# First attention of a hybrid layer on one Trainium2 core: order of the square roots, the scan's top by doubling passes, x summed in PSUM, search constants made earlier

## The chip, the core and the metric

The kernel runs on one core of one Trainium2 chip. Its time is the device time of one execution in microseconds (us), measured over several runs. Next to it stands one profiled execution, from which all rows below are taken. A core has five engines with a queue each: PE (TensorE, matrix multiply, with its weight loads shown as PEld), DVE (VectorE), ACT (ScalarE), POOL (GpSimd) and SP (SyncE, which only issues DMAs). Each runs its own list of instructions in order, and they meet only through semaphores.

## The reference

x has the shape (2, 2048, 128). Four layers are added to it in turn: a first attention with a complex linear recurrence, an expert layer, a linear attention, and the expert layer again; each sees the layer norm of x. The change touches only the first:

```
a2 = (xf @ w_a.T).reshape(b, l, inner, 2)
a_mag2 = a2[..., 0] ** 2 + a2[..., 1] ** 2
a = complex(a2) * (rsqrt(a_mag2) * sigmoid(log(a_mag2)))
xc = complex(x2) * (rsqrt(x_mag2) * x_mag2)
u = einsum('mn,bln->blm', inv(V), roll(xc, h0))
_, s = associative_scan(combine, (a, a * u), axis=1)    # s[t] = a[t] * s[t-1] + a[t] * u[t]
h = einsum('mn,bln->blm', V, s) + xc
x = x + h.real @ w_out.T
```

The expert layer that follows needs a layer norm of the new x, so mean and variance of every row, and a search for the 256 tokens of each expert, which walks over the bits of a threshold.

## The kernel before, in words

Sizes in the code: NB = 2 sequences of LT = 2048 positions, D = 128, INNER = 64, GW = 512 positions per block, NK = 4 blocks, NG = 8 groups of 512 rows of x, LEVELS = 11. The recurrence is laid out with one channel per partition (64 channels of each sequence, 128 partitions) and time along the free dimension; real and imaginary part are planes of one tile. `av` holds a, `XC` holds xc, `SS` the scan's values, `lev` the products of a over 2, 4, 8, ... positions.

Startup: x is loaded (`load_x`), VectorE makes the statistics, `scales` turns them into mean and 1/deviation, and `norm_a` normalises 32 tiles (L1056). After that VectorE does `coefficients(k)` for the four blocks (L1098 to L1021).

Block loop (NK times): TensorE projects a block (L770, two halves), with one step of a Newton iteration for the inverse of V in between (`inverse`). ScalarE copies the projection out of PSUM (L562, `raw`), runs its part of the inverse (L531, L535, L539, L541), keeps the next block's transposed x (`keep_xT`, L521) and squares (L569). `roots(k-1)` (L553) takes the square roots of the magnitudes of the block before; it is called after the first half's copy and `keep_xT`. VectorE's `coefficients(k)` waits for `squared`, adds squares to magnitudes (L1098, `mag_ready`), makes a reciprocal (L1101), waits for `rooted`, and multiplies; the last product raises `proj_used`.

GpSimd forms the products of a by pairs (`level`, L395 to L398): two levels for each block (`BY_BLOCK`), then levels 3 to 10 over the whole length. A level is four instructions: two with a pair of planes each, two with one plane. A block's levels wait for `proj_used` of the block and `mag_ready` of the next one. Every level raises `lev_ready`.

After the coefficients VectorE makes the search's constants (`bits`, ten small instructions, L1021 and L1025, each waiting for the one before). Then comes the scan. `times` is its complex product: two products of two planes each, a subtraction and an addition of one plane, and, where it adds to what is there, one addition of two planes; five instructions of L1021 in that case. First five chunks (two of 256 positions, three of 512) make the lowest level out of u, which TensorE puts into PSUM (L796 to L799). Then levels 1 to 10 go up the tree, and 9 to 0 down it, each as one `times` or two. Level n has LT / 2^(n+1) products. The last one, level 0 going down, has 1023, in two parts of 512 and 511; each part raises `s_ready`.

Way out: for eight groups of 256 positions TensorE adds up in PSUM bank n the contribution of xc (first loop, `way_out(.., 2, ..)`, started once `u_used` is complete) and of the scan (second loop, L807, waiting for `s_ready`, 1 for the first four groups and 2 for the others), and raises `ao_ready`. VectorE adds each group to x (`row`, `xs`), raises `x1_ready`, and makes four statistics (L1175). SP waits for all of `x1_ready` before it stores x for the expert layer.

What each line number stands for in the rows: L1021 is the helper `tt`, any two-input operation of VectorE; L1025 and L1026 are the helper `ts`. A float32 matmul shows as two passes (x2).

Of the kernel before, what the change touches and what calls it, by code (L numbers as in the profile page):

```python
# [10 lines left out]
ALU = mybir.AluOpType  # L11
# [26 lines left out]
def build(nc, x, wa, wx, wo, vr, vi, vrT, viT, h0r, h0i, wqkvT, woutT, nw, rwT, rb, f1T, f1b, f2T, f2b, out):  # L38
# [30 lines left out]
    with ExitStack() as ctx:  # L69
# [45 lines left out]
        rt2 = tbf[:, 2 * GW:4 * GW].rearrange("p (c t) -> p c t", c=2)  # L115
        rec = tbf[:, 4 * GW:5 * GW]

        MB = tbf[:, 3600:3600 + 3 * 2 * D].rearrange("p (i b d) -> p i b d", i=3, b=NB)
        T1 = sq[:, 0:2, :]
        T2 = sq[:, 2:4, :]  # L120
# [133 lines left out]
        AT_ROOT, AT_FIRST, AT_STEP = 8, 12, 6  # L254

        BY_BLOCK = 2
        lv_at = [0] * (LEVELS + 1)
        for lv in range(2, LEVELS):
            lv_at[lv] = lv_at[lv - 1] + (LT >> (lv - 1))
# [88 lines left out]
        def _(pool):  # L348
# [38 lines left out]

            scratch = stage.rearrange("p j d -> p (j d)")

            def level(A, B, n):  # L390
# [3 lines left out]
                even, odd = A[:, :, 0::2], A[:, :, 1::2]  # L394
                G.did(pool.tensor_tensor(t1, odd[:, 0:1, :].to_broadcast([P, 2, n]), even, ALU.mult))  # L395
                G.step(pool.tensor_tensor(t2, odd[:, 1:2, :].to_broadcast([P, 2, n]), even, ALU.mult))
                G.did(pool.tensor_tensor(B[:, 0, :], t1[:, 0, :], t2[:, 1, :], ALU.subtract))
                pool.tensor_tensor(B[:, 1, :], t1[:, 1, :], t2[:, 0, :], ALU.add).then_inc(lev_ready, 1)  # L398
                G.settle()

            for k in range(NK):

                pool.wait_ge(proj_used, k + 1)
                if k + 1 < NK:
                    pool.wait_ge(mag_ready, k + 2)
                pool.wait_ge(transposed, min(2 * (k + 2), NG))
                A = av[:, :, k * GW:(k + 1) * GW]
                for i in range(BY_BLOCK):
                    n = GW >> (i + 1)
                    B = lev[:, :, lv_at[i + 1] + k * n:lv_at[i + 1] + (k + 1) * n]  # L410
                    level(A, B, n)
                    pool.wait_ge(lev_ready, k * BY_BLOCK + i + 1)
                    A = B
            for lv in range(BY_BLOCK + 1, LEVELS):
                n = LT >> lv
                level(lev[:, :, lv_at[lv - 1]:lv_at[lv - 1] + 2 * n], lev[:, :, lv_at[lv]:lv_at[lv] + n], n)
                pool.wait_ge(lev_ready, level_done(lv))

            def feed(f):

# [84 lines left out]
        def _(act):  # L505
# [51 lines left out]
                keep_xT(0, b, b * NK)  # L557
            for k in range(NK):
                at = AT_FIRST + AT_STEP * k
                for i, raw in enumerate((av[:, :, k * GW:(k + 1) * GW], XC[:, :, 1 + k * GW:1 + (k + 1) * GW])):  # L560
                    act.wait_ge(projected, 2 * k + i + 1)
                    nc.scalar.activation(raw, ps[:, 2 * i:2 * i + 2, :], ACT.Copy).then_inc(raw_ready, 1)  # L562
                    inverse(at + 2 * i + 1)
                    if k + 1 < NK:
                        keep_xT(0, 2 * (k + 1) + i, i * NK + k + 1)
                    if i == 0 and k >= 1:
                        roots(k - 1)
                    act.wait_ge(raw_ready, 2 * k + i + 1)
# [15 lines left out]
            for b, r in enumerate((lo_, hi_)):  # L584
                nc.scalar.activation(MB[r, 0, b, :], ps[r, 7, 0:D], ACT.Copy)
                last = nc.scalar.activation(MB[r, 1, b, :], ps[r, 7, D:2 * D], ACT.Copy, scale=-1.0)
            last.then_inc(mt_ready, 1)

            def feed(f):
                run = 1 + 2 * f  # L590
# [111 lines left out]
        def _(pe):  # L702
# [107 lines left out]
            for n in range(2 * NK):  # L810
                for t in range(2):
                    at = (2 * n + t) * P + 1
                    way_out(n, t, 2, XC[:, 0, at:at + P])
            for n in range(2 * NK):
                pe.wait_ge(s_ready, 1 if n < NK else 2)
                for t in range(2):
                    at = (2 * n + t) * P
                    for i in range(2):
                        last = way_out(n, t, i, SS[:, i, at:at + P])
                last.then_inc(ao_ready, 1)  # L820
# [196 lines left out]
        def _(dve):  # L1017
# [91 lines left out]

            for k in range(NK):  # L1110
                norm_a(k)
            for k in range(NK):
                coefficients(k)
            def times(cr, ci, n, q, o, add_to, done=None, count=0):
# [15 lines left out]
                    V.step(tt(to[:, 1, :], t1[:, 1, :], t2[:, 0, :], ALU.add))  # L1130


            dve.wait_ge(consts, 3)
            V.step(tt(bits[:, 0:32], ione[:, :], ish[:, :], ALU.logical_shift_left))
            low, shifted = bits[:, 32:33], bits[:, 33:34]
            V.step(tt(low, bits[:, 1:2], bits[:, 2:3], ALU.bitwise_or))
            for by in (2, 4, 8, 16):
                V.step(ts(shifted, low, by, None, ALU.logical_shift_right))
                V.step(tt(low, low, shifted, ALU.bitwise_or))
            for c, (t0, w) in enumerate(U_CHUNKS):  # L1140
                H = w // 2
                dve.wait_ge(u_ready, c + 1)
# [5 lines left out]
                tt(v, SS[:, :, e], U[:, :, 1::2], ALU.add).then_inc(u_used, 1)  # L1148
                dve.wait_ge(u_used, c + 1)
                times(av[:, 0:1, o], av[:, 1:2, o], H, v, SS[:, :, o], False)  # L1150
            for lv in range(1, LEVELS):
                s, n = 1 << lv, LT >> (lv + 1)
                dve.wait_ge(lev_ready, level_done(lv))
                A = lev[:, :, lv_at[lv]:lv_at[lv] + 2 * n]
                for c0 in range(0, n, GW):
                    w = min(GW, n - c0)
                    q = SS[:, :, s - 1 + c0 * 2 * s::2 * s][:, :, 0:w]
                    o = SS[:, :, 2 * s - 1 + c0 * 2 * s::2 * s][:, :, 0:w]
                    times(A[:, 0:1, 2 * c0 + 1::2][:, :, 0:w], A[:, 1:2, 2 * c0 + 1::2][:, :, 0:w], w, q, o, True)
            for lv in range(LEVELS - 2, -1, -1):  # L1160
                s, n = 1 << lv, (LT >> (lv + 1)) - 1
                A = lev[:, :, lv_at[lv]:lv_at[lv] + 2 * (n + 1)] if lv else av
                for c0 in range(0, n, GW):
                    w = min(GW, n - c0)
                    q = SS[:, :, 2 * s - 1 + c0 * 2 * s::2 * s][:, :, 0:w]
                    o = SS[:, :, 3 * s - 1 + c0 * 2 * s::2 * s][:, :, 0:w]
                    times(A[:, 0:1, 2 * c0 + 2::2][:, :, 0:w], A[:, 1:2, 2 * c0 + 2::2][:, :, 0:w], w, q, o, True,
                          s_ready if lv == 0 else None, c0 // GW + 1)
# [282 lines left out]
```

## Time and profile before

| | us |
|---|---|
| median of 3 runs | 735.89 (734.93 to 737.31) |
| the profiled execution | 735.69 |
| its span | 733.9 |
| busy: PE, DVE, POOL, ACT | 410.8, 461.8, 355.6, 205.2 |

The profile's span is the time from the first to the last instruction of the program; the execution's time has a little around it. In a row of the chain or of the timeline the first number is the start in us from the span's start, the second how long it took (several instructions when "xN" stands behind it), then the engine, the tile written and the source line. In the chain a piece is listed until the next piece takes over.

### The profile page before, as it was taken

To read this page: it belongs to the slowest core of one execution; us is meant where nothing else is said; L and a number is where in the kernel's file an instruction comes from. 1 tells how busy PE (TensorE), PEld (TensorE's weight loads), DVE (VectorE), ACT (ScalarE), POOL (GpSimd) and SP (SyncE) were. 2 spreads that over 40 slices of the span, in tenths; PEclk is the share of its full clock that TensorE was granted. 3 is DMA by queue.
4 is the path that set the end of the run, shared out by engine and by line. 5 is a ranking of instruction groups with operands and counts; after the bars stand their busy time and mean duration, and the time that the engine had idled before them with its cause. 6 is when DMAs were issued, how large, how long until landed. Compare 5 with 4: busy or idle time off the path is not lost.

```text
span 733.9 us, 7537 instructions
## 1 busy us (share of the span) xinstructions
PE 410.8 (56%) x2130; PEld 273.7 (37%) x2130; DVE 461.8 (63%) x1199; ACT 205.2 (28%) x487; POOL 355.6 (48%) x350
## 2 busy tenths in 40 slices
PE   4887560084231396674057888887753313975650
PEld 4554140072110286664023433433331102965540
DVE  6779999997778322222439899999777783222210
ACT  2575000003440142222064334333234401422210
POOL 5048930002000478887308788888720004688853
PEclk9999886589555599998559899999975555999885
DMA  5950000006002523334700000000060024233322
GB/s 139 364 225 0 0 1 0 0 0 172 0 0 52 136 51 47 45 38 64 201 0 0 1 0 2 0 1 0 1 171 1 0 60 130 40 46 44 45 23 18
DMA packets 49860, 38.91 MB, mean 53 GB/s; under 512 B 8672, under 2 KB 46176, under 8 KB 48544
## 3 DMA queue, kind: packets, MB, share of 16 engines
q1 hardware_dynamic: 36000, 28.30, 12.6%
q0 software_dynamic: 11392, 9.05, 9.3%
q10 hardware_dynamic: 2432, 1.11, 0.6%
q8 instruction: 17, 0.28, 0.2%
q14 instruction: 19, 0.16, 0.1%
HBM read 22.73 MB, written 15.73 MB: 52 GB/s over the span
## 4 chain that ended last, share of the span: by engine, by line
DVE 27%; POOL 22%; issue 17%; DMA 15%; PE 13%; ACT 4%; SPq 1%; DVEq 1%; ACTq 0%; POOLq 0%
DVE arena L1021 10%; POOL tb L501 8%; DMA out<-arena,idx 5%; DMA acc<-arena,idx 5%; POOL acc L455 4%; POOL out L455 4%; POOL arena L442 3%; DVE tk L1026 2%; PE ps L807 2%; DVE arena L1026 2%; PE ps L770 2%; DVE tb L1056 2%; DMA tab<-tb 2%; PE ps L855 2%; POOL arena L497 1%
## 5 line engine op out<-in xcount | busy, mean ns | idle before, releaser
L1021 DVE TENSOR_TENSOR arena<-ps,arena 128x256 f32<-128x256 f32 (+1 forms) x36 | 16.4, 454 | 139.6 <-DMA acc<-arena,idx 59.5
L615 ACT ACTIVATE arena<-ps,b 128x256 f32<-128x256 f32 x128 | 50.1, 474 | 143.7 <-PE ps L907 143.7
L501 POOL TENSOR_TENSOR tb<-arena 128x512 f32<-128x512 f32 x64 | 80.4, 1270 | 17.2 <-DVE arena L1369 17.2
L954 PE MATMUL ps<-xT,arena 128*128 128x512 f32 x128 | 71.7, 654 | 20.7 <-DVE arena L1369 20.6
L907 PE MATMUL ps<-arena,f1w 128*128 128x256 f32 x256 | 73.3, 438 | 17.6 <-DVE arena L1025 12.7
L442 POOL DMA_INDIRECT arena<-tab,idx x64 | 62.6, 978 | 41.5 <-DMA tab<-tb 22.6
L917 PEld LDWEIGHTS ps<-f2w,arena 128*128 128x128 f32 x512 | 64.2, 197 | 4.4 <-issue 2.2
L917 PE MATMUL ps<-f2w,arena 128*128 128x128 f32 x512 | 63.9, 279 | 2.0 <-DVE arena L1025 2.0
L907 PEld LDWEIGHTS ps<-arena,f1w 128*128 128x128 f32 x256 | 53.8, 221 | 27.4 <-DVE arena L1025 14.4
L455 POOL DMA_INDIRECT out<-arena,idx x32 | 50.9, 1590 | 23.5 <-issue 10.5
L271 POOL DMA_DIRECT2D arena<-cntd x4 | 2.7, 687 | 117.3 <-DMA cntd<-arena 117.3
L1021 DVE TENSOR_TENSOR arena<-arena 128x256 f32<-128x256 f32 (+26 forms) x127 | 57.8, 490 | 2.6
L455 POOL DMA_INDIRECT acc<-arena,idx x32 | 50.6, 1580 | 9.7 <-issue 7.0
L807 PE MATMUL ps<-tb,arena 128*128 128x256 f32 x96 | 25.4, 433 | 44.1 <-DVE arena L1021 37.8
L423 POOL CAST arena<-ident 128x128 f16<-128x128 f32 x2 | 0.6, 289 | 83.1 <-DVE tb L1056 83.1
L1026 DVE TENSOR_SCALAR_CACHE_REDUCE arena<-arena,tk 128x320 f16<-128x320 f32 (+1 forms) x66 | 37.1, 564 | 4.7 <-DVE tk L1026 2.1
L807 PEld LDWEIGHTS ps<-tb,arena 128*128 128x128 f32 x96 | 21.1, 222 | 48.8 <-DVE arena L1021 38.2
L604 ACT ACTIVATE arena<-arena,tk 128x192 f16<-128x192 f32 x60 | 27.3, 455 | 42.2 <-DVE tk L1026 40.0
L954 PEld LDWEIGHTS ps<-xT,arena 128*128 128x128 f32 x128 | 22.1, 205 | 45.5 <-DVE arena L1369 38.2
L517 ACT ACTIVATE sd<-sd 128x32 f32<-128x32 f32 x4 | 0.9, 227 | 133.5 <-DVE sd L1044 133.5
L1369 DVE TENSOR_TENSOR_SCAN arena<-ones,arena,ps 128x512 f32<-128x512 f32 x30 | 37.3, 1261 | 0.0
L891 PE MATMUL ps<-ident,arena 128*128 128x128 f32 x64 | 14.4, 311 | 37.8 <-DMA arena<-tab,idx 29.9
(230 smaller groups left out, 936.8 us busy)
## 6 DMA issues: line engine op xcount, KB each, us to landing
tab<-tb SPq DMA_DIRECT2D x8, 576.0 KB, 5.7
f1w<-in_f1T SPq DMA_DIRECT2D x4, 1024.0 KB, 12.5
f2w<-in_f2T SPq DMA_DIRECT2D x4, 1024.0 KB, 14.3
acc<-tb SPq DMA_DIRECT2D x8, 256.0 KB, 18.7
arena<-in_f2b SPq DMA_DIRECT2D x2, 1024.0 KB, 6.0
acc<-xs SPq DMA_DIRECT2D x8, 256.0 KB, 6.5
xs<-acc SPq DMA_DIRECT2D x8, 256.0 KB, 5.8
arena<-acc SPq DMA_DIRECT2D x8, 256.0 KB, 5.4
```

The lines of the kernel that those rows point to most:

```text
L442: pool.indirect_dma_start(out=XE[:, e % RX, h, :], out_offset=None, in_=tab[f], in_offset=bass.IndirectOffsetOnAxis(ap=idx[:, i:i + 1], ax ...
L455: pool.indirect_dma_start(out=outf if f else acc[e % 2], out_offset=bass.IndirectOffsetOnAxis(ap=idx[:, i:i + 1], axis=0), in_=yv[:, e % 2 ...
L501: pool.tensor_tensor(QS[:, i, :], ST[:, r, i, :], qn[:, r, :], ALU.mult).then_inc(qs_ready, 1)
L604: nc.scalar.activation(eq[:, DCOL:GW], even[:, DCOL:GW], ACT.Sign, bias=tk[:, 0:1], scale=-1.0, accum_out=sg[:, 0:1]).then_inc(signed, 1)
L615: last = nc.scalar.activation(hT[:, e % 2, t, :], ps[:, 2 * (e % 2) + t // 2, (t % 2) * CAP:(t % 2 + 1) * CAP], ACT.Gelu, bias=b1[:, e, t: ...
L807: return nc.tensor.matmul(ps[:, n, t * 2 * D:(t + 1) * 2 * D], lhs, MB[:, i, :, :].rearrange("p b d -> p (b d)"), start=(i == 2 and t == 0 ...
L907: last = nc.tensor.matmul(ps[:, 2 * (e % 2) + t // 2, (t % 2) * CAP:(t % 2 + 1) * CAP], f1w[:, e, t * P:(t + 1) * P], xeT[:, e % 2, :], st ...
L917: last = nc.tensor.matmul(ps[:, 6 + m % 2, h * P:(h + 1) * P], hT[:, m % 2, t, h * P:(h + 1) * P], f2w[:, m, t, :], start=(t == 0), stop=( ...
L954: nc.tensor.matmul(ps[:, u % V_BANKS, :], WV[:, i, :, :].rearrange("p h a -> p (h a)"), xT[:, n * GW:(n + 1) * GW], start=True, stop=True) ...
L1021: return nc.vector.tensor_tensor(o, a, b, op)
L1026: return nc.vector.tensor_scalar(o, a, s1, s2, op0, op1, **kw)
L1369: nc.vector.tensor_tensor_scan(ST[:, r, i, :], ones_in.to_broadcast([P, GW]), kv, ST[:, 1 - r, i, GW - 1:GW] if n % NK else 0.0, ALU.mult, ...
```

## The change

Four edits.

- ScalarE: `roots(k-1)` is called ahead of the copy of a block's first half, where it was called behind it.
- VectorE: the search's constants are made behind `norm_a`, ahead of `coefficients`, where they were made behind these.
- The scan's top: with TOP = 6 there are NTOP = 32 values left. VectorE goes up by levels 1 to 5, then makes five passes with strides 1, 2, 4, 8, 16 over the 32 values (widths 31, 30, 28, 24, 16), then down by levels 5 to 0. GpSimd makes levels 3 to 6, and then the coefficients of the passes in four steps, kept in `over_top`. The last level (0, down) is cut into four parts of 256 and 255, and `s_ready` counts to four.
- The way out: a matmul of the identity with the rows of x joins each group and half in the first loop. ScalarE copies the finished groups out of PSUM over x and raises `x1_ready`; VectorE only makes the statistics.

```
@@ gpsimd
-            for lv in range(BY_BLOCK + 1, LEVELS):
+            for lv in range(BY_BLOCK + 1, TOP + 1):
                 n = LT >> lv
-                level(lev[:, :, lv_at[lv - 1]:lv_at[lv - 1] + 2 * n], lev[:, :, lv_at[lv]:lv_at[lv] + n], n)
+                A = lev[:, :, lv_at[lv - 1]:lv_at[lv - 1] + 2 * n]
+                level(A[:, :, 0::2], A[:, :, 1::2], lev[:, :, lv_at[lv]:lv_at[lv] + n], n)
                 pool.wait_ge(lev_ready, level_done(lv))
+            for j, d in enumerate(STRIDES[:-1]):
+                A = over_top[j]
+                level(A[:, :, d:NTOP - d], A[:, :, 2 * d:NTOP], over_top[j + 1][:, :, 2 * d:NTOP], NTOP - 2 * d)
+                pool.wait_ge(lev_ready, level_done(TOP + j + 1))
@@ scalar
+                if k >= 1:
+                    roots(k - 1)
                 for i, raw in enumerate((av[:, :, k * GW:(k + 1) * GW], XC[:, :, 1 + k * GW:1 + (k + 1) * GW])):
                     act.wait_ge(projected, 2 * k + i + 1)
                     nc.scalar.activation(raw, ps[:, 2 * i:2 * i + 2, :], ACT.Copy).then_inc(raw_ready, 1)
                     inverse(at + 2 * i + 1)
                     if k + 1 < NK:
                         keep_xT(0, 2 * (k + 1) + i, i * NK + k + 1)
-                    if i == 0 and k >= 1:
-                        roots(k - 1)
...
+            for n in range(2 * NK):
+                act.wait_ge(ao_ready, n + 1)
+                nc.scalar.activation(xrows[:, :, 2 * n:2 * n + 2, :], ps[:, n, :].rearrange("p (t b d) -> p b t d", t=2, b=NB),
+                                     ACT.Copy).then_inc(x1_ready, 1)
@@ tensor
                     way_out(n, t, 2, XC[:, 0, at:at + P])
+                    nc.tensor.matmul(ps[:, n, t * 2 * D:(t + 1) * 2 * D], ident[:, :], xrows[:, :, 2 * n + t, :],
+                                     start=False, stop=False, skip_group_check=True)
             for n in range(2 * NK):
-                pe.wait_ge(s_ready, 1 if n < NK else 2)
+                pe.wait_ge(s_ready, n // 2 + 1)
@@ vector (the ten instructions on bits, between norm_a and coefficients now)
...
-            for lv in range(1, LEVELS):
+            for lv in range(1, TOP):
...
-            for lv in range(LEVELS - 2, -1, -1):
+            for j, d in enumerate(STRIDES):
+                dve.wait_ge(lev_ready, level_done(TOP + j))
+                w, s, A = NTOP - d, 1 << TOP, over_top[j]
+                ends = SS[:, :, s - 1::s]
+                times(A[:, 0:1, d:], A[:, 1:2, d:], w, ends[:, :, 0:w], ends[:, :, d:], True)
+            for lv in range(TOP - 1, -1, -1):
...
-                for c0 in range(0, n, GW):
-                    w = min(GW, n - c0)
+                part = GW if lv else GW // 2
+                for c0 in range(0, n, part):
+                    w = min(part, n - c0)
...
             for n in range(2 * NK):
-                dve.wait_ge(ao_ready, n + 1)
-                row = xs[:, :, :].rearrange("p (b j) d -> p b j d", b=NB)[:, :, 2 * n:2 * n + 2, :]
-                tt(row, row, ps[:, n, :].rearrange("p (t b d) -> p b t d", t=2, b=NB), ALU.add).then_inc(x1_ready, 1)
                 dve.wait_ge(x1_ready, n + 1)
```

## Rows read from the trace of the kernel before

**Rows 1.** The page, part 4: shares of the chain that ended last, by engine.
```profile
DVE 27%; POOL 22%; issue 17%; DMA 15%; PE 13%; ACT 4%; SPq 1%; DVEq 1%; ACTq 0%; POOLq 0%
```

**Rows 2.** Chain of waits in time, 64 to 79 us: start, us, engine, tile, line.
```profile
64.50 1.39 DVE tb L1098
...
74.05 0.37 DVE bits L1021
...
78.92 0.76 DVE arena L1021 x2
```

**Rows 3.** Windows: stretch, length, PE, PEld, DVE, ACT, POOL busy (instructions), PEclk, DMA, GB/s.
```profile
28.70:33.07 4.37, 3.73 (x24) 2.21 (x20) 0.00 (x0) 3.40 (x8) 0.00 (x0) 1.00 1.02 424
...
74.90:98.50 23.60, 12.91 (x24) 5.10 (x24) 22.67 (x43) 0.00 (x0) 21.45 (x40) 0.86 0.00 0
```

**Rows 4.** Timeline, all engines, 24 to 39 us; in brackets idle time before, and releaser.
```profile
24.41 1.94 PE L770 MATMUL ps<-xT,waT 128*64 128x512 f32 x8 [0.78 <-ACT xT L521]
...
33.07 1.23 DVE L1098 TENSOR_TENSOR tb<-arena 128x1024 f32<-128x1024 f32 x1 [4.38 <-ACT arena L569]
...
35.09 1.94 PE L770 MATMUL ps<-xT,waT 128*64 128x512 f32 x8
35.19 0.28 ACT L541 ACTIVATE XX<-ps 128x128 f32<-128x128 f32 x1
...
37.07 1.02 ACT L562 ACTIVATE arena<-ps 128x1024 f32<-128x1024 f32 x1 [1.60 <-PE ps L770]
...
38.63 1.06 ACT L553 ACTIVATE tb<-tb 128x1024 f32<-128x1024 f32 x1
```

**Rows 5.** Groups by form, VectorE, 73.9 to 103.9 us: busy us, mean ns, idle.
```profile
L1021 DVE TENSOR_TENSOR bits<-bits 128x1 uint32<-128x1 uint32 x5 | 3.5, 710 | 0.2
...
L1025 DVE TENSOR_SCALAR bits<-bits 128x1 uint32<-128x1 uint32 x4 | 0.6, 154 | 0.1
```

**Rows 6.** Timeline of VectorE: chunks 0, 1 and 4, and one small instruction.
```profile
81.26 1.93 DVE L1021 TENSOR_TENSOR arena<-arena,tb 128x256 f32<-128x256 f32 x2
...
84.69 0.75 DVE L1021 TENSOR_TENSOR arena<-arena,ps 128x256 f32<-128x256 f32 x2
...
99.20 1.29 DVE L1021 TENSOR_TENSOR arena<-arena,ps 128x512 f32<-128x512 f32 x2
100.52 0.76 DVE L1021 TENSOR_TENSOR arena<-arena 128x256 f32<-128x256 f32 x2
...
185.72 0.16 DVE L1021 TENSOR_TENSOR tk<-tk,bits 128x1 uint32<-128x1 uint32 x1
```

**Rows 7.** Chain of waits, the tree: level 1 up, 3 up, 5 up, 6 up, 5 down.
```profile
104.17 3.97 DVE arena L1021 x2
...
116.70 0.51 DVE arena L1021 x2
...
119.38 0.46 DVE arena L1021 x2
...
120.49 0.35 DVE arena L1021 x2
...
127.66 0.45 DVE arena L1021 x2
```

**Rows 8.** Chain of waits: last level going down, and the last statistics.
```profile
143.81 2.37 DVE arena L1021 x2
...
165.99 0.88 DVE bst L1175 x4
```

**Rows 9.** Windows: the first 4 us of the way out, columns as in rows 3.
```profile
148.80:152.80 4.00, 3.99 (x9) 3.20 (x10) 3.93 (x5) 0.00 (x0) 0.00 (x0) 0.50 0.00 0
```

**Rows 10.** Timeline: the way out's two loops on TensorE, a copy on ScalarE.
```profile
38.15 0.60 ACT L521 ACTIVATE xT<-ps 128x512 f32<-128x512 f32 x1
...
102.06 9.00 PE L807 MATMUL ps<-tb,arena 128*128 128x256 f32 x32 [6.31 <-DVE tb L1021]
148.81 16.42 PE L807 MATMUL ps<-tb,arena 128*128 128x256 f32 x64 [37.75 <-DVE arena L1021]
```

More of the change, by code:

```diff
@@ L116, in build @@
         rec = tbf[:, 4 * GW:5 * GW]
+        xrows = xs[:, :, :].rearrange("p (b j) d -> p b j d", b=NB)
         MB = tbf[:, 3600:3600 + 3 * 2 * D].rearrange("p (i b d) -> p i b d", i=3, b=NB)
@@ L256, in build @@
         BY_BLOCK = 2
+        TOP = 6
+        NTOP = LT >> TOP
+        STRIDES = [1 << j for j in range(NTOP.bit_length() - 1)]
+        over_top = [lev[:, :, sum(LT >> i for i in range(1, TOP)):][:, :, 0:NTOP]]
+        over_top += [tbf[:, 2560 + 2 * NTOP * j:2560 + 2 * NTOP * (j + 1)].rearrange("p (c t) -> p c t", c=2)
+                     for j in range(len(STRIDES) - 1)]
         lv_at = [0] * (LEVELS + 1)
@@ L388, in _, with level @@
             scratch = stage.rearrange("p j d -> p (j d)")
-            def level(A, B, n):
+            def level(even, odd, B, n):
                 t1 = scratch[:, 0:2 * n].rearrange("p (c t) -> p c t", c=2)
                 t2 = scratch[:, 2 * n:4 * n].rearrange("p (c t) -> p c t", c=2)
-                even, odd = A[:, :, 0::2], A[:, :, 1::2]
                 G.did(pool.tensor_tensor(t1, odd[:, 0:1, :].to_broadcast([P, 2, n]), even, ALU.mult))
@@ L410, in _ @@
                     B = lev[:, :, lv_at[i + 1] + k * n:lv_at[i + 1] + (k + 1) * n]
-                    level(A, B, n)
+                    level(A[:, :, 0::2], A[:, :, 1::2], B, n)
                     pool.wait_ge(lev_ready, k * BY_BLOCK + i + 1)
                     A = B
-            for lv in range(BY_BLOCK + 1, LEVELS):
+            for lv in range(BY_BLOCK + 1, TOP + 1):
                 n = LT >> lv
-                level(lev[:, :, lv_at[lv - 1]:lv_at[lv - 1] + 2 * n], lev[:, :, lv_at[lv]:lv_at[lv] + n], n)
+                A = lev[:, :, lv_at[lv - 1]:lv_at[lv - 1] + 2 * n]
+                level(A[:, :, 0::2], A[:, :, 1::2], lev[:, :, lv_at[lv]:lv_at[lv] + n], n)
                 pool.wait_ge(lev_ready, level_done(lv))
+            for j, d in enumerate(STRIDES[:-1]):
+                A = over_top[j]
+                level(A[:, :, d:NTOP - d], A[:, :, 2 * d:NTOP], over_top[j + 1][:, :, 2 * d:NTOP], NTOP - 2 * d)
+                pool.wait_ge(lev_ready, level_done(TOP + j + 1))
             def feed(f):
@@ L1111, in _ @@
                 norm_a(k)
+            dve.wait_ge(consts, 3)
+            V.step(tt(bits[:, 0:32], ione[:, :], ish[:, :], ALU.logical_shift_left))
+            low, shifted = bits[:, 32:33], bits[:, 33:34]
+            V.step(tt(low, bits[:, 1:2], bits[:, 2:3], ALU.bitwise_or))
+            for by in (2, 4, 8, 16):
+                V.step(ts(shifted, low, by, None, ALU.logical_shift_right))
+                V.step(tt(low, low, shifted, ALU.bitwise_or))
             for k in range(NK):
@@ L1130, in times @@
                     V.step(tt(to[:, 1, :], t1[:, 1, :], t2[:, 0, :], ALU.add))
[L1133 to L1139, printed above, removed]
             for c, (t0, w) in enumerate(U_CHUNKS):
@@ L1167, in _ @@
                     times(A[:, 0:1, 2 * c0 + 2::2][:, :, 0:w], A[:, 1:2, 2 * c0 + 2::2][:, :, 0:w], w, q, o, True,
-                          s_ready if lv == 0 else None, c0 // GW + 1)
+                          s_ready if lv == 0 else None, c0 // part + 1)
             for n in range(2 * NK):
-                dve.wait_ge(ao_ready, n + 1)
-                row = xs[:, :, :].rearrange("p (b j) d -> p b j d", b=NB)[:, :, 2 * n:2 * n + 2, :]
-                tt(row, row, ps[:, n, :].rearrange("p (t b d) -> p b t d", t=2, b=NB), ALU.add).then_inc(x1_ready, 1)
                 dve.wait_ge(x1_ready, n + 1)
```

## Prediction

> **What bounds the kernel now.** I read the page first. The chain of work that ended last is shared out over VectorE, GpSimd, DMA and TensorE [rows 1], so no engine bounds the whole and each edit has to be judged in its own stretch. All edits lie in the first attention, the first 167 us. So the second view is the chain of waits in order of time over that stretch. It shows the kernel changing its limit three times.
>
> Up to 64.5 us the block loop (projection, square roots, matrix inverse) sets the pace. TensorE starts a block's first projection at 24.41 and the next block's at 35.09, that is 10.68 us later [rows 4], and the two blocks behind follow at the same distance. From 64.5 to 148.8 us the chain is VectorE alone: coefficients of the last block, the search constants, five chunks of the scan's lowest level, and the tree up and down [rows 2, 7, 8]. From 148.8 to 165.3 it is TensorE's way out, 64 passes in 16.42 us [rows 10], and then one addition, four statistics instructions [rows 8] and the normalising. Behind that comes the first expert layer. Its search, gathers and scatters start from these statistics through semaphores alone, so I let what is won here pass through to the end one for one.
>
> **Square roots first in a block.** ScalarE ends block 0's last copy at 35.19 + 0.28 = 35.47 and then idles until the projection lands (copy at 37.07); today the root sits behind that copy, at 38.63 [rows 4]. The magnitudes it needs are done at 33.07 + 1.23 = 34.30 [rows 4]. After the change the root runs at 35.5 to 36.5, inside the idle time, 0.5 us before the copy is due. VectorE gets its roots some 2 us earlier. Its next multiplication can then start when the reciprocal ends (about 38.2 instead of 39.8). But the pace is not set there. Block 0 holds no root and takes the same 10.68 us as the blocks that hold one, and the last block's magnitudes start at 64.50 [rows 2], right behind ScalarE's squares, whatever VectorE did before. I cost this edit at **0**. What hides the root is the 1.6 us before the copy; without that cover each of three blocks would lose up to 1.06 us. The added head-of-line risk is ScalarE waiting for magnitudes with the copy, the inverse's copies and the kept xT queued behind it. The slack there is 35.47 - 34.30 = 1.2 us plus the 0.5 us.
>
> **Search constants behind the normalising.** Ten small VectorE instructions move from 74.05-78.92 [rows 2], where they are on the chain and cost 4.87 us, to the gap 28.70 to 33.07, where VectorE is wholly idle and so is GpSimd [rows 3]. Undisturbed, such an instruction takes 0.16 us [rows 6], with 0.02-0.03 us between, so ten take about 2.0 us and end near 30.7. They fit, and normalising is ahead of them.
>
> Taking them out does not return all 4.87 us. The instructions with two inputs took 710 ns on average and those with one 154 ns [rows 5], because GpSimd's tree levels run there; it is busy 21.45 us of 74.90-98.50 [rows 3]. Excess of the constants: 4.87 - 2.0 = 2.9 us. The chunks behind them suffer too. An undisturbed long chunk is 104.17 - 99.20 = 4.97 us [rows 6, 7]. A short one, from undisturbed pairs of the same widths (0.75, 0.51, half of 0.75, 0.76, 0.51 and five gaps of 0.02) [rows 6, 7], is 3.0. Five chunks undisturbed: 2 x 3.0 + 3 x 4.97 = 20.9. They took 104.17 - 78.92 = 25.25, so 4.35 us of excess; chunk 0 alone has 84.69 - 78.92 - 3.0 = 2.8 [rows 2, 6]. GpSimd's heavy work stays where it is in time (its last block starts only when GpSimd ends the one before), so the chunks move forward into it. Chunk 0 now meets what the constants met (I take 2.7 of their 2.9), chunk 1 what chunk 0 met (2.3 of 2.8, since more of it now reads PSUM while GpSimd's long instructions run), chunk 2 a part of what chunk 1 met (0.7). That is 5.7 us of excess, the chunks end at 74.05 + 20.9 + 5.7 = 100.65 instead of 104.17, and the edit brings **3.5 us**. Bounds: 4.87 if the chunks suffer no more than today, 2.0 if the whole 2.9 + 4.35 = 7.25 us stays lost. The pair that GpSimd hits hardest shows why it will not be the upper end: 1.93 us against 0.76 [rows 6].
>
> The Trainium skill (GPSIMD Engine Reference, Specifications) says GpSimd shares SBUF interfaces with VectorE and contends with VectorE instructions that read two SBUF inputs. By that rule, which the one-input rows bear out with their 154 ns, the edit pays less than the 4.87 us that the chain shows; taken as a full return the gain below would be 1.4 us larger.
>
> **The scan's top.** Levels 6 to 10 going up and 9 to 6 going down, nine in all, stand in the chain from 120.49 to 127.66, 7.17 us [rows 7]. They are small and cost their fixed part. Five doubling passes of width 31, 30, 28, 24 and 16 take their place, each of five instructions as a level has. The level of width 32 takes 120.49 - 119.38 = 1.11 us and the mean of the nine, of 16 and less, is 0.80 [rows 7]; between them I take 1.10 + 1.09 + 1.06 + 1.02 + 0.92 = 5.2. Gain **2.0 us**; bounds 1.6 (all at 1.11) and 3.2 (all at 0.80). On GpSimd four steps of width 30 to 16 replace four of 16 to 2. That ends near 99 as before [rows 3], while VectorE asks for the first of them at about 117, so it is hidden with 17 us to spare.
>
> **The last level in four parts.** Its first half takes 148.81 - 143.81 = 5.0 us [rows 8] and releases TensorE, which has been waiting. A quarter is two products of 512 elements (1.29), two halves of 256 (0.76), one addition of 512 (half of 1.29) and gaps: 2.8 us [rows 6]. TensorE starts **2.1 us** earlier against that clock. Four quarters cost VectorE 11.1 us instead of 9.9, but nothing waits for that: TensorE needs 4.1 us for the two groups of a quarter on average, and even in the faster part (16.42 - 4.0) / (64 - 9) x 16 = 3.6 us [rows 9, 10], more than 2.8, so it never starves. The statistics, 0.88 us a group [rows 8], catch up with 2 us a group. Bounds: 0 and 2.4.
>
> The skill speaks against this cut (VectorE: DVE Perf Modes, "The TRN2 errata"): each instruction pays a fixed latency, so tiles of 512 or more elements are advised. Ten more instructions are 1.2 us here, agreeing with the rule, and would count if VectorE were the limit of this stretch; then this part would lose 1.2 rather than win 2.1.
>
> **x summed by TensorE.** Sixteen matmuls, 32 passes, join the 32 of 102.06 [rows 10], at most at the same 9.0 us. They start near 98.6 and end by 117, and the quarter is ready at 141: 24 us of cover, without which they cost 9.0. The additions leave VectorE and eight ScalarE copies come in; a copy of 512 elements out of PSUM takes 0.60 [rows 10]. ScalarE has nothing queued but the root of the next statistics, which waits for them anyway. Only the last one counts. Today the last statistics start at 165.99, 0.76 behind the end of the way out at 148.81 + 16.42 [rows 8, 10]; then it is 0.60 and two hops of 0.03 to 0.05. **0**, bounds -0.2 to +0.2. Storing x starts at the same distance from the way out.
>
> **Sum.** 3.5 + 2.0 + 2.1 = 7.6 us. Against the profiled execution: span 733.9, time 735.69, giving 728.1; the median of the runs, 735.89, is 0.2 above it, so **728.2**.
>
> **The rivals.** (1) *The port keeps its whole toll*: the constants bring only 2.0; 5.5 to 6.1 in all, 729.8. For it: the excess belongs to GpSimd's 21 us more than to the victim. Against: part of a chunk reads PSUM and was not slowed. (2) *It returns all*: 4.9, with the top at its better end, 726.5. (3) *The early start is lost*: 730.3, if TensorE's first quarter meets the lower clock longer. In 148.80-152.80 its granted clock is 0.50, which is 1.2 GHz, behind 37.7 us without work [rows 9, 10]; the idle time will now be about 24 us, and I expect the same start. (4) *The roots hold up the blocks*: 3 x 1.06, 731.4; it decides once magnitudes come 1.7 us later than now. (5) *TensorE starves between quarters and stays at the lower clock*: 64 passes at 4.0/9 = 0.44 us are 28 us, which the boundary passes counted short make nearer 26, so 9 to 10 us lost, 737.5. It decides when a quarter takes over 3.6 us; it is estimated at 2.8 and GpSimd is idle then. This is also the case in which the quarters do not do what they say. (6) *Slower*: VectorE and GpSimd run strictly one after the other from 74 to 98.5. VectorE would lose up to GpSimd's 21.45 us instead of 5.7, 15.8 more: 744.0. It decides from about 10 us of excess more than I took. Today the excess is 7.25 in the same stretch with the same GpSimd work, which speaks against it.
>
> **How the numbers follow.** Forecast 0.58, (1) 0.16, (2) 0.09, (3) 0.05, (4) 0.02, together 0.90 faster by over 0.3% (2.2 us, about what a measurement of this kernel can tell from no change). (5) is within 0.3%: 0.06. (6) is slower: 0.04. The range takes in the bounds: all terms near their best, 4.9 + 2.7 + 2.4 = 10.0, gives 725.9; constants at 2.0 and no early start, 4.0, gives 731.9. Range 725.8 to 732.0, with (5), (6) and a little more outside.
>
> **What the profile after would show.** VectorE's ten constants at about 28.7-30.7, each two-input one near 0.16 us; roots in front of the projection's copy, blocks still 10.7 us apart and the last magnitudes at 64.5; chunks from 74.1 to 100.7; no level between widths 32 and 16 but five passes of about 1.05 us; way out starting 2.8 us after the last level does, near 141, and taking 16.4 us; last statistics ended near 159.2 instead of 166.9. It is wrong if the chunks end after 102.5, if the blocks are more than 10.9 us apart, if the way out has gaps between its groups, or if the stretch behind the statistics is not as long as before.

## The result and the profile after

The kernel before took 735.99 us in this comparison (median of 4), the changed one 728.89 (727.53 to 729.38). The ratio is 0.9887, with a 95% interval from 0.9866 to 0.9907: faster by 1.1%, or 7.1 us between the medians. The forecast was 728.2 with a range of 725.8 to 732.0.

The span of the profiled execution went from 733.9 to 727.2 us. The shares of the chain on the page after, where VectorE had 27% and TensorE 13% before [rows 1]:

```profile
span 727.2 us, 7592 instructions
...
DVE 24%; POOL 20%; issue 16%; PE 16%; DMA 14%; ACT 4%; SPq 2%; DVEq 1%; ACTq 0%; POOLq 0%
```

Three points are some 20 us, more than the edits moved, so the shares don't measure them. Most of TensorE's rise lies behind the statistics, in a stretch that is as long as before. Some of it lies ahead of the first chunk, where the chain below now names a matmul of u (L816) as what came last. VectorE's own last product was as late (71.93 + 1.64 = 73.57), and in experiment 7 the first chunk starts at 72.47, ahead of that matmul at 73.02. So VectorE's order still sets this start.

The chain of waits of the changed kernel (start, us, engine, tile, line; L1117 is the last block's magnitudes, L1040 VectorE's two-input helper, L824 the way out, L816 a matmul of u, L603 the new ScalarE copy, L1197 the statistics) answers rows 2, 7 and 8:

```profile
64.16 1.24 DVE tb L1117
...
72.98 0.45 PE ps L816 x2
73.49 0.75 DVE arena L1040 x2
...
101.19 3.98 DVE arena L1040 x2
...
118.70 0.44 DVE arena L1040 x2
...
138.91 1.30 DVE arena L1040 x2
...
141.79 16.45 PE ps L824 x64
158.25 0.61 ACT xs L603
158.86 0.03 issue
158.88 0.88 DVE bst L1197 x4
159.77 0.02 issue
159.79 0.47 DVE sd L1040 x3
```

Read as distances, these give the whole gain up to the statistics' last step (before it stood at 166.90, which is the 0.88 us piece of [rows 8] and a hop behind 165.99):

| stretch | before | after | difference | forecast |
|---|---|---|---|---|
| start to the last magnitudes | 64.50 | 64.16 | -0.34 | 0 |
| magnitudes to the end of the coefficients | 9.55 | 9.33 | -0.22 | 0 |
| constants (before only) and five chunks | 30.12 | 27.70 | -2.42 | -3.5 |
| level 1 up to the last level down | 39.64 | 37.72 | -1.92 | -2.0 |
| last level to the way out's start | 5.00 | 2.88 | -2.12 | -2.1 |
| way out | 16.42 | 16.43 | 0 | 0 |
| its end to `scales` | 1.67 | 1.57 | -0.10 | 0 |
| sum, at `scales` | 166.90 | 159.79 | -7.11 | -7.6 |
| `scales` to the end | 567.0 | 567.4 | +0.4 | 0 |

The 0.34 us at the start is no effect of the edits. The first 26 us are one program in both kernels, and the first block's first copy starts at 26.38 before and 26.04 after, so the 0.34 us is there already. The runs below show last magnitudes anywhere from 64.08 to 64.95. In the timeline after (columns as in [rows 6]) the constants stand in the gap and take 0.15 to 0.18 us each:

```profile
28.27 0.18 DVE L1040 TENSOR_TENSOR bits<-ione,ish 128x32 uint32<-128x32 uint32 x1
28.48 0.16 DVE L1040 TENSOR_TENSOR bits<-bits 128x1 uint32<-128x1 uint32 x1
28.68 0.15 DVE L1044 TENSOR_SCALAR bits<-bits 128x1 uint32<-128x1 uint32 x1
```

### The profile page after: what moved, and what is told of

Its sections match the earlier page's. It is cut to its first block, busy times and chain, and to the rows that moved or that the text cites. A ratio compares the mean times of both kernels' runs of the same rounds, so it can differ in the third digit from the quotient of the medians.

```text
span 727.2 us, 7592 instructions
## 1 busy us (share of the span) xinstructions
PE 415.1 (57%) x2162; PEld 278.8 (38%) x2162; DVE 456.2 (63%) x1181; ACT 210.2 (29%) x495; POOL 356.9 (49%) x350
## 4 chain that ended last, share of the span: by engine, by line
DVE 24%; POOL 20%; issue 16%; PE 16%; DMA 14%; ACT 4%; SPq 2%; DVEq 1%; ACTq 0%; POOLq 0%
DVE arena L1040 10%; POOL tb L513 8%; DMA out<-arena,idx 6%; POOL acc L467 4%; POOL out L467 4%; DMA acc<-arena,idx 4%; DVE tk L1045 2%; PE ps L926 2%; PE ps L824 2%; DVE arena L1045 2%; PE ps L787 2%; DVE tb L1075 2%; DMA tab<-tb 2%; PE ps L874 2%; PE ps L936 1%
## 5 line engine op out<-in xcount | busy, mean ns | idle before, releaser
L1040 DVE TENSOR_TENSOR arena<-ps,arena 128x256 f32<-128x256 f32 (+1 forms) x36 | 16.3, 454 | 140.0 <-DMA out<-arena,idx 58.9
L926 PE MATMUL ps<-arena,f1w 128*128 128x256 f32 x256 | 71.8, 431 | 17.4 <-DVE arena L1044 12.9
L973 PE MATMUL ps<-xT,arena 128*128 128x512 f32 x128 | 68.7, 631 | 20.1 <-DVE arena L1391 20.1
L1040 DVE TENSOR_TENSOR arena<-arena 128x256 f32<-128x256 f32 (+21 forms) x109 | 57.4, 560 | 2.2
L824 PE MATMUL ps<-tb,arena 128*128 128x256 f32 x96 | 27.0, 421 | 32.8 <-DVE arena L1040 27.1
L973 PEld LDWEIGHTS ps<-xT,arena 128*128 128x128 f32 x128 | 21.4, 197 | 43.6 <-DVE arena L1391 36.1
L824 PEld LDWEIGHTS ps<-tb,arena 128*128 128x128 f32 x96 | 20.2, 213 | 37.3 <-DVE arena L1040 27.5
L509 POOL TENSOR_TENSOR arena<-arena 128x512 f32<-128x512 f32 x24 | 30.5, 1271 | 5.8 <-ACT arena L691 5.6
```

Of the source, the lines that this page charges most:

```text
L509: pool.tensor_tensor(KV[:, j % 2, :], KV[:, j % 2, :], kn[:, r, :], ALU.mult).then_inc(kv_ready, 1)
L824: return nc.tensor.matmul(ps[:, n, t * 2 * D:(t + 1) * 2 * D], lhs, MB[:, i, :, :].rearrange("p b d -> p (b d)"), start=(i == 2 and t == 0 ...
L926: last = nc.tensor.matmul(ps[:, 2 * (e % 2) + t // 2, (t % 2) * CAP:(t % 2 + 1) * CAP], f1w[:, e, t * P:(t + 1) * P], xeT[:, e % 2, :], st ...
L973: nc.tensor.matmul(ps[:, u % V_BANKS, :], WV[:, i, :, :].rearrange("p h a -> p (h a)"), xT[:, n * GW:(n + 1) * GW], start=True, stop=True) ...
L1040: return nc.vector.tensor_tensor(o, a, b, op)
```

## The experiments

The expectations were written before the runs. Times are medians; the ratio is to the kernel before on the same chip. The spread from run to run of one kernel is 2 to 8 us, wider than most terms. It goes with TensorE's mean granted clock: of the 17 executions of the kernel before that stand beside experiments 1 to 4, the five shortest (734.7 to 736.0 us) had 0.784 to 0.788 and the five longest (738.5 to 739.6) had 0.773 to 0.780. No run of the changed kernel stands beside the experiments, so against it the ratios are compared, and two such ratios leave some 2 us open either way. That can't decide between most of the theories below. The traces decide, in the distances of the table. From the last magnitudes to `scales` the changed kernel has 95.63 us and the kernel before 102.40.

**1. Constants back behind the coefficients** (the wait and the ten instructions on `bits`), all else as changed.

```
             for k in range(NK):
                 norm_a(k)
-            dve.wait_ge(consts, 3)
-            ...
             for k in range(NK):
                 coefficients(k)
...
+            dve.wait_ge(consts, 3)
+            ...
             for c, (t0, w) in enumerate(U_CHUNKS):
```

> The changed kernel with the ten search constants back behind the coefficients. Theory (the chunks moved forward into GpSimd's heavy work and pay its toll in the constants' place): the stretch from the last coefficient to level 1, 27.7 us in the changed kernel, becomes about 30.1, so 2.4 us slower than the changed kernel. Rival A, that the constants' whole 4.9 us came back and something else took 2.5: 4.9 slower, some 32.6 us. Rival B, that the gap they were put in was not free: under 1.5.

733.88 us, ratio 0.9951 (0.9932 to 0.9970). Last coefficient to level 1: 104.59 - 74.26 = 30.33 us, against 27.70. So the constants are worth 2.6 us there, not 4.9. The time alone would have spoken for rival A: by the ratios this kernel is 4.7 us behind the changed one. From the magnitudes to `scales` the trace has 3.3 of them. Besides the 2.6, another 0.6 us came from a way out of 17.06 us instead of 16.43. This is a difference of TensorE's low-clock start, told of below, and not of the edit.

**2. Square roots back behind the copy.**

```
             for k in range(NK):
                 at = AT_FIRST + AT_STEP * k
-                if k >= 1:
-                    roots(k - 1)
...
                         keep_xT(0, 2 * (k + 1) + i, i * NK + k + 1)
+                    if i == 0 and k >= 1:
+                        roots(k - 1)
```

> The changed kernel with the square roots again behind the copy and the kept xT. Theory: blocks stay 10.69 us apart, the last magnitudes start 31.36 us behind the second block's (64.16 - 32.80 in the changed kernel), the reciprocal is followed by 1.6 us of idle VectorE, and the time moves by 0 to 0.3 us. Rival (the root in front of the copy costs or wins block time): 1 to 3 us either way, with another distance between blocks.

730.78 us, ratio 0.9904 (0.9881 to 0.9927). That interval overlaps the changed kernel's. The timelines of both on ScalarE show the same pace, 10.69 and 10.70 us from the projection's copy of one block to the next (L574 and L576). First this run, with the root (L565) behind the copy, then the changed kernel:

```profile
37.16 1.02 ACT L574 ACTIVATE arena<-ps 128x1024 f32<-128x1024 f32 x1 [1.60 <-PE ps L787]
38.72 1.06 ACT L565 ACTIVATE tb<-tb 128x1024 f32<-128x1024 f32 x1
...
47.85 1.03 ACT L574 ACTIVATE arena<-ps 128x1024 f32<-128x1024 f32 x1 [1.60 <-PE ps L787]
```

```profile
35.03 1.05 ACT L565 ACTIVATE tb<-tb 128x1024 f32<-128x1024 f32 x1
36.73 1.02 ACT L576 ACTIVATE arena<-ps 128x1024 f32<-128x1024 f32 x1 [0.66 <-PE ps L787]
...
47.43 1.02 ACT L576 ACTIVATE arena<-ps 128x1024 f32<-128x1024 f32 x1 [0.42 <-PE ps L787]
```

The root only used up ScalarE's idle time before the copy, 1.60 down to 0.66 us. Magnitudes to `scales` is 95.83 us here, 0.2 more than the changed kernel. Most of that is a last magnitudes instruction of 1.38 us instead of 1.23, which GpSimd's block before still met.

**3. The last level in two parts.**

```
-                part = GW if lv else GW // 2
+                part = GW
...
-                pe.wait_ge(s_ready, n // 2 + 1)
+                pe.wait_ge(s_ready, n // 4 + 1)
```

> The changed kernel with the last level of the scan in parts of 512 and 511 and TensorE waiting for two of them. Theory: the way out starts 5.0 us behind the level's start where it is 2.88, takes the same 16.4, and the kernel is 2.1 us slower. Rival (the quarter's start is taken back, since TensorE starts at the lower clock anyway and is then held up by VectorE's longer level): under 0.7 slower, with a way out of over 17 us in the changed kernel's place.

732.51 us, ratio 0.9935 (0.9919 to 0.9952). The way out starts 143.85 - 138.84 = 5.01 us behind the level's start and takes 16.79. From the level's start to `scales` it is 23.37 us against 20.88, so 2.1 us of start and 0.4 of a longer start at the lower clock. The first theory holds. The ratios say 3.5 us, with the uncertainty above.

**4. x added by VectorE again**, quarters kept.

```
-                    nc.tensor.matmul(ps[:, n, t * 2 * D:(t + 1) * 2 * D], ident[:, :], xrows[:, :, 2 * n + t, :], ...)
...
-                act.wait_ge(ao_ready, n + 1)
-                nc.scalar.activation(xrows[:, :, 2 * n:2 * n + 2, :], ps[:, n, :]..., ACT.Copy).then_inc(x1_ready, 1)
...
+                dve.wait_ge(ao_ready, n + 1)
...
+                tt(row, row, ps[:, n, :]..., ALU.add).then_inc(x1_ready, 1)
                 dve.wait_ge(x1_ready, n + 1)
```

> The changed kernel with x added by VectorE again, no identity matmuls and no ScalarE copies. Theory: TensorE's last pass still sets the end; only the tail behind it differs, 0.69 us of addition for 0.60 of copy and a hop, so 0.0 to 0.1 us slower. Rival (with the quarters VectorE's 11.4 us level plus eight groups of 1.6 us is 24 us, longer than 2.9 + 16.4): the tail becomes VectorE's, about 4 to 5 us slower than the changed kernel. The rival follows from the sum of the rows and would make this edit a part without which the quarters win nothing.

733.65 us, ratio 0.9949 (0.9928 to 0.9969), by the ratios 4.6 us behind the changed kernel. The rival holds in kind: VectorE is the last. Its timeline (L1034 addition, L1194 statistics), the first group and the last two:

```profile
150.36 0.69 DVE L1034 TENSOR_TENSOR xs<-xs,ps 128x512 f32<-128x512 f32 x1
151.08 0.87 DVE L1194 BATCH_NORM_STATS2 bst<-xs 128x6 f32<-128x128 f32 x4
...
159.34 0.67 DVE L1034 TENSOR_TENSOR xs<-xs,ps 128x512 f32<-128x512 f32 x1
160.04 0.87 DVE L1194 BATCH_NORM_STATS2 bst<-xs 128x6 f32<-128x128 f32 x4
160.83 0.67 DVE L1034 TENSOR_TENSOR xs<-xs,ps 128x512 f32<-128x512 f32 x1
161.53 0.87 DVE L1194 BATCH_NORM_STATS2 bst<-xs 128x6 f32<-128x128 f32 x4
```

No idle time stands between them; TensorE was through at 141.83 + 16.04 = 157.87. From the level's start (138.95) to `scales` (162.44) it takes 23.49 us. In the kernel before, with halves, it is 23.09, and in the changed kernel 20.88. So the quarters alone would win nothing, and the x edit is worth 2.6 us with them. The rival's 4 to 5 was too high for two reasons: a group takes 1.50 us and not 1.6, and the last group's share of VectorE stands behind TensorE's line too. Up to the last group VectorE needs 11.4 + 7 x 1.5 = 21.9 us and TensorE 2.9 + 16.4 = 19.3, and the difference is the 2.6. The profiled execution lost another 2.7 us behind `scales` (570.1 against 567.4). The windows there, first the changed kernel, then this one at the same distance behind `scales`, show a lower granted clock (0.97 and 0.87, the third number from the end):

```profile
409.80:459.80 50.00, 43.08 (x182) 20.64 (x182) 47.85 (x68) 21.93 (x42) 42.13 (x34) 0.97 0.00 1
```

```profile
412.40:462.40 50.00, 44.93 (x178) 20.35 (x178) 45.83 (x65) 19.53 (x36) 38.83 (x33) 0.87 0.00 1
```

Why it was lower stays open; no experiment shows an edit's hand in it.

**5. The plain tree back**, quarters kept: `TOP`'s passes out, `range(1, LEVELS)` and `range(LEVELS - 2, -1, -1)` on VectorE, GpSimd's levels to 10.

> The changed kernel with the plain tree again (levels 1 to 10 up, 9 to 0 down, GpSimd's levels 3 to 10), quarters and the rest kept. Theory: four small levels more, the stretch from level 1 to the last level 39.6 us where it is 37.7, so 1.9 slower. Rival (the passes also spare something on GpSimd or behind): over 3 or under 1 slower.

737.55 us on a chip where the kernel before took 742.64; ratio 0.9935 (0.9917 to 0.9952), which in this ratio is 3.5 us behind the changed kernel. The trace puts level 1 to the last level at 141.09 - 101.44 = 39.65 us, that is 1.93 more. The stretch from magnitudes to `scales` is 96.63 us, only 1.0 more, as its way out took 15.70. What the ratio has beyond that is not in the attention; it is about what two ratios leave open, and no trace here explains it.

**6. The kernel before with only the constants moved.**

> The kernel before with only the ten search constants moved behind the normalising. Theory: the stretch from the last coefficient to level 1 goes from 30.1 to about 27.6, so 2.5 us faster than before and no more, though the chain of before showed 4.87 us on them. Rival A: 4.9 faster. Rival B (needs the roots first): under 1 faster.

739.87 us, ratio 0.9955 (0.9938 to 0.9973), 3.3 us faster. Last coefficient to level 1: 101.95 - 74.44 = 27.51 us against 30.12, so 2.6. Together with experiment 1 and the table, the move is worth 2.4 to 2.6 us in this stretch, with or without the other edits. Rival A is out, and so is rival B.

**7. GpSimd fills zeros where it made products** (the products of a are left out, so the scan is another).

```
             def level(even, odd, B, n):
-                ...
+                pool.memset(B, 0.0).then_inc(lev_ready, 1)
```

> The changed kernel, where GpSimd fills each level's result with zeros in one instruction in place of four products; the products of a are left out, so the scan's result is another. Theory (GpSimd's products hold up VectorE's two-input instructions): the five chunks take 20.9 us where they take 27.7, and the multiplications of the coefficients 1.23, 0.69 and 1.23 where they take 1.5, 1.2 and 1.6. Rival (the chunks are long by themselves, or by TensorE's reads): above 25 us. The kernel is 7 to 9 us faster by the first theory.

One execution, 727.95 us; the kernel before takes 742.64 on that chip. The chunks run from 72.47 to 93.53, 21.06 us, against 27.70. The groups by form between 73 and 93 us show which instructions were held. First the changed kernel, then this one (us busy, mean ns):

```profile
L1040 DVE TENSOR_TENSOR arena<-arena 128x128 f32<-128x128 f32 x8 | 4.7, 630 | 0.1
L1040 DVE TENSOR_TENSOR arena<-arena,tb 128x256 f32<-128x256 f32 x4 | 3.7, 965 | 0.1
...
L1040 DVE TENSOR_TENSOR arena<-arena,ps 128x512 f32<-128x512 f32 x4 | 2.6, 685 | 0.1
```

```profile
L1036 DVE TENSOR_TENSOR arena<-arena,ps 128x512 f32<-128x512 f32 x6 | 3.9, 684 | 0.1
...
L1036 DVE TENSOR_TENSOR arena<-arena 128x128 f32<-128x128 f32 x8 | 2.0, 289 | 0.1
L1036 DVE TENSOR_TENSOR arena<-arena,tb 128x256 f32<-128x256 f32 x4 | 1.5, 422 | 0.1
```

With both inputs in SBUF, an instruction of 256 elements falls from 965 to 422 ns and one of 128 from 630 to 289. With one input in PSUM it stays at 685 and 684. So the 6.6 us are GpSimd's products'. The filling itself held up nothing: between 72.66 and 74.97 it ran beside pairs of 0.49 and 0.76 us, which are undisturbed values (line L402, then VectorE).

```profile
72.66 2.31 POOL L402 MEMSET arena<- 128x512 f32 x6 [5.78 <-issue]
...
73.25 0.49 DVE L1036 TENSOR_TENSOR arena<-arena 128x128 f32<-128x128 f32 x2
...
74.24 0.76 DVE L1036 TENSOR_TENSOR arena<-arena,tb 128x256 f32<-128x256 f32 x2
```

The coefficients' multiplications fell too, from 1.49, 1.21 and 1.64 us to 1.23, 0.68 and 1.22.

**8. The same, with the constants back.**

> The same, GpSimd filling zeros (the products of a left out), and the ten search constants behind the coefficients again. Theory: they take 2.0 us there, 0.16 each, so the stretch from the last coefficient to level 1 is 22.9 us against 20.9. Rival (the constants are slow for what they are): 4.9 us.

729.88 us in one execution. The constants start at 72.37 and the first chunk at 74.32, 1.95 us; the chunks end at 95.38.

```profile
72.79 0.15 DVE L1040 TENSOR_SCALAR bits<-bits 128x1 uint32<-128x1 uint32 x1
72.98 0.16 DVE L1036 TENSOR_TENSOR bits<-bits 128x1 uint32<-128x1 uint32 x1
```

Without GpSimd's products the constants cost 2.0 us where the chain of before gave them 4.87.

**9. Passes one level lower** (TOP = 5: 64 values, six passes; their coefficients in a place of `tbf` that is free by then).

> The changed kernel with the passes one level lower (64 values, six passes of width 63, 62, 60, 56, 48 and 32, levels 1 to 4 around them). Theory (a pass costs what a level of its width costs, read from the rows): levels 5 up and down, 2.2 us, and five passes, 5.15, are replaced by six passes of 8.1 to 8.4, so the stretch from level 1 to the last level is 0.8 to 1.1 us longer than 37.7 and the kernel up to 1 us slower. Rival (instructions cost a flat 0.2 us and their number counts, five fewer): 0.5 faster.

732.71 us, ratio 0.9939 (0.9914 to 0.9963). Level 1 to the last level: 140.54 - 101.86 = 38.68 us, 0.96 more than the changed kernel, as the first theory has it. The stretch from magnitudes to `scales` is 97.78 us, 2.15 more, and by the ratios the kernel is 3.8 us behind, more than the theory's 1. A pass costs what a level of its width costs; the count of instructions alone does not set it. The chunks became 0.6 us longer too (28.33), which I hadn't expected: up to 91 us both timelines are alike, and then GpSimd's wider steps, which now end at 101.54 and not at 98.89, fall into the last two chunks. The other 0.6 us is a way out of 17.00.

**10. The first quarter halved.**

```
+                cuts = [0, 128, 256, 512, 768, n] if lv == 0 else list(range(0, n, GW)) + [n]
...
-                pe.wait_ge(s_ready, n // 2 + 1)
+                pe.wait_ge(s_ready, n + 1 if n < 2 else n // 2 + 2)
```

> The changed kernel with the first quarter of the last level cut once more, parts of 128, 128, 256, 256, 255, TensorE's first two groups waiting for one part each. Theory: a part of 128 takes 1.8 us, so the way out starts 1.8 behind the level's start where it is 2.9, and the time falls by 1.1 us. Rival (TensorE starves behind the first part or VectorE becomes the limit by its level and statistics, 12.0 + 7.2 = 19.2 against 1.8 + 16.4 + 1.5 = 19.7): under 0.5.

728.91 us, ratio 0.9883 (0.9860 to 0.9906): no difference from the changed kernel that this can tell. The way out started 141.01 - 139.20 = 1.81 us behind the level's start, as expected, but took 16.82 us, so 0.7 us is left at `scales`. TensorE did not starve, as its 64 passes stand in the timeline without a gap; its clock rose later. In the sixth microsecond of the way out (146.01 to 147.01) the granted clock is 0.72, where the changed kernel has 1.00 from the start of its sixth (146.79) on.

**11. Level 3 block by block, and no wait for the next magnitudes.**

```
-        BY_BLOCK = 2
+        BY_BLOCK = 3
...
-                if k + 1 < NK:
-                    pool.wait_ge(mag_ready, k + 2)
```

> The changed kernel with GpSimd making level 3 block by block too, and starting a block without waiting for the next one's magnitudes. Theory (the toll is GpSimd's two-input work in the stretch of the chunks, and some of it can lie earlier): GpSimd has 2.7 us less to do behind 74 us, the chunks end 0.5 to 1.5 us earlier; GpSimd's third block meets the last block's magnitudes, up to 0.3 us back. Rival (GpSimd's total work sets it, wherever it lies before level 1): no gain, or a loss where the products slow the coefficients.

728.66 us, ratio 0.9891 (0.9859 to 0.9922), again no difference. The chunks took 100.61 - 74.22 = 26.39 us, 1.3 less. The coefficients in front of them grew by 0.4 us (74.22 - 64.47 = 9.75): GpSimd's third block now starts at 64.70, and an instruction of VectorE with one input (L1117, at 65.73) is held by it. GpSimd's product, then VectorE's groups by form, 64 to 70 us, in this kernel and in the kernel before:

```profile
64.70 2.13 POOL L402 TENSOR_TENSOR stage<-arena 128x512 f32<-128x512 f32 x1
```

```profile
L1117 DVE TENSOR_SCALAR tb<-tb 128x512 f32<-128x512 f32 x1 | 1.4, 1379 | 0.0
```

```profile
L1100 DVE TENSOR_SCALAR tb<-tb 128x512 f32<-128x512 f32 x1 | 0.4, 426 | 0.0
```

**12. Experiments 10 and 11 together.**

> The last two together. Theory: they lie in different stretches and add up, 1.6 to 2.6 us faster than the changed kernel. Rival: the gain of one is what is seen.

728.58 us, ratio 0.9884 (0.9865 to 0.9902). In the trace, magnitudes to `scales` is 158.36 - 64.19 = 94.17 us, 1.5 us shorter than the changed kernel. The two add up there (0.7 and 0.6 alone), but a gain of 1.5 us is under what these runs can tell. It is no better version that the times show.

## Why the prediction was right, step by step

**What bounds it** held. The last magnitudes stand right behind ScalarE's squares, blocks are 10.69 us apart, and all the gain is made up to `scales`. It passes through: 567.4 us behind it, against 567.0.

**Square roots: 0** held (experiment 2: 0.2 us, by a contended instruction that now runs free).

**Search constants: 3.5** was the mis-sized term; it measured 2.4. The kind was right, and experiments 7 and 8 show it. The undisturbed values of the prediction, 20.9 us for the chunks and 2.0 for the constants, came out as 21.06 and 1.95. The step that failed is the share that I let the chunks escape. I put their excess at 5.7 us, and it was 27.70 - 21.06 = 6.6 of the 30.12 - 21.06 - 1.95 = 7.1 that constants and chunks had lost together. The first two chunks came as forecast (2.6 and 2.5 us of excess over its 3.0, where 2.7 and 2.3 stood). The miss is behind them: chunk 3 had been given no excess and had 0.2, and chunk 2 had been given 0.7. In the timeline after it runs from 84.60 to 90.96, 6.36 us, 1.4 above the undisturbed 4.97, because its pairs with two SBUF inputs meet GpSimd's level 4 (from 85.98 on) and level 5 (from 89.33 on):

```profile
84.60 1.29 DVE L1040 TENSOR_TENSOR arena<-arena,ps 128x512 f32<-128x512 f32 x2
85.92 1.29 DVE L1040 TENSOR_TENSOR arena<-arena 128x256 f32<-128x256 f32 x2
87.24 0.69 DVE L1040 TENSOR_TENSOR tb<-arena,ps 128x512 f32<-128x512 f32 x1
87.96 1.77 DVE L1040 TENSOR_TENSOR arena<-arena,tb 128x512 f32<-128x512 f32 x2
```

So rival (1), the port keeps its toll, was nearer the truth than the forecast: nearly all the excess stayed, and what the move brought is the constants' own 2.0 us and little more.

**The scan's top: 2.0** measured 1.92, and 1.93 in experiment 5. The five passes run from 117.60 to 122.76 in the chain after, 5.16 us, where 5.2 was put.

**The last level in quarters: 2.1** measured 2.12 at the way out's start. The quarter itself took 2.88 us; with the 2.8 of its working the difference would have been 2.2. That the way out then took the same time in both profiles, 16.42 and 16.43 us, is luck: over all profiled executions it took 15.69 to 17.06.

**x summed by TensorE: 0** was wrong as a term, though the sum came out. I priced the edit beside halves. There, up to the last group, TensorE's 5.0 + 16.4 = 21.4 is longer than VectorE's 9.9 + 7 x 1.5 = 20.4 with little to spare. With quarters VectorE's line is 21.9 and TensorE's 19.3 (experiment 4). "The statistics catch up" is true only when the additions have left. Experiment 4 shows 2.6 us lost without the edit. From the level's start to `scales` it is 23.09 us before, 23.37 with the x edit alone (experiment 3), 23.49 with quarters alone (experiment 4) and 20.88 with both: they have one gain between them and neither has it alone. Sums of edits priced one by one hide such a pair. The cover of the identity matmuls was ample: they ended at 114.7, against a way out at 141.8.

**The sum**, 7.1 at `scales` against 7.6, came out nearer than its largest term, in part by luck. The constants fell 1.1 us short. Against that, 0.34 us came from an earlier start that no edit made, and 0.3 us from the coefficients and the tail, both put at nothing.

**The rivals.** (2) is out by experiments 1 and 6. (3), (4) and (5) did not come: the way out has no gaps and took 16.43 us. (6) did not come either: of GpSimd's 21 us VectorE lost 6.6.

## What to carry to other kernels

Work taken off a chain that runs beside a contending engine may return its undisturbed cost and not the time that the chain shows. Here 4.87 us of constants returned 2.4, near their undisturbed 2.0, as the contention fell on what moved into their place. It is no fixed toll, though: with part of GpSimd's work moved earlier (experiment 11) the chunks got 1.3 us shorter and the coefficients only 0.4 longer. Before an early start for one engine is counted, add up the line of the engine behind it as well, with all edits in place. Here that line was 2.6 us too long until its additions went elsewhere.

## What the runs showed of the hardware

A product of GpSimd held up VectorE instructions with both inputs in SBUF, by up to the length of its own: 128x128 elements took 289 ns alone and 630 on average beside it, and 1 element 0.16 us alone and up to 1.17 beside it. The 1.17 us end when GpSimd's product does, at 76.2 (kernel before):

```profile
75.01 1.17 DVE L1021 TENSOR_TENSOR bits<-bits 128x1 uint32<-128x1 uint32 x1
```

```profile
74.91 1.26 POOL L395 TENSOR_TENSOR stage<-arena 128x512 f32<-128x512 f32 x1
```

It goes the other way too: a product of GpSimd of 128x256 elements took 0.73 us at 49.46 in the kernel before, with VectorE idle, and 1.52 us at 49.13 in the changed kernel, where a product of VectorE ran from 48.54 to 50.07. VectorE instructions with one input in PSUM were not held (684 and 685 ns), and GpSimd's filling held none (experiment 7). One input is no protection by itself: a scalar operation on 128x1 stayed at 154 ns [rows 5], but the one on 128x512 went from 426 to 1379 ns when a GpSimd product ran at its start. The Trainium skill (GPSIMD Engine Reference, Specifications) says that GpSimd contends with VectorE instructions in a 2-port performance mode or with two SBUF inputs. The second case is what experiment 7 shows; the 1379 ns agree with the first, though no run here shows the mode.

The same 64 passes of the way out took between 15.69 and 17.06 us. In the changed kernel, behind 27.1 us without work on TensorE, the first 4 us had a granted clock of 0.50 (1.2 GHz) and the part from 149.70 on had 1.00 (2.4 GHz):

```profile
141.70:145.70 4.00, 3.91 (x9) 3.20 (x10) 3.86 (x8) 0.10 (x1) 0.00 (x0) 0.50 0.00 0
145.70:149.70 4.00, 4.00 (x18) 3.40 (x17) 3.83 (x9) 1.19 (x3) 0.00 (x0) 0.89 0.00 0
149.70:158.25 8.55, 8.52 (x40) 7.16 (x38) 6.41 (x29) 2.92 (x5) 0.00 (x0) 1.00 0.00 1
```

How long the lower level lasts differs from one profiled execution to the next. Experiment 5, with 15.70 us, had 0.86 in the fourth microsecond of its way out; experiment 1, with 17.06, had 0.50 in its sixth:

```profile
146.96:147.96 1.00, 1.00 (x5) 0.83 (x5) 1.00 (x2) 0.36 (x1) 0.00 (x0) 0.86 0.00 0
```

```profile
150.20:151.20 1.00, 1.00 (x4) 0.82 (x3) 0.97 (x2) 0.00 (x0) 0.00 (x0) 0.50 0.00 0
```

That is up to 1.4 us of way out, more than some of the edits tried here could win. What sets it no run shows.
